# Row scores of both attentions made ten heads ahead, their maxima turned in two parts, and the first stage of the program put in another order

## The chip, the cores and the metric

One core of one Trainium2 chip runs the whole program. The metric is the device time of one execution in microseconds (us), start to end; lower is better. The kernel before was timed in three runs.

## The reference, cut to what matters

Input x is 8 x 100 x 256 (800 rows), the context is 8 x 361 x 256. Four blocks follow each other, each added to x with a gate: an attention, a feed-forward block with fake quantisation, a second attention, and a mixture of eight experts.

```
x = x + tanh(g_xattn[0]) * attention0(layernorm(x), ctx)      # 16 heads of 16, keys: own 100 rows + 361 of the context
x = x + tanh(g_ffn[0])   * quantised_ffn(layernorm(x))        # 256 -> 704 -> 256
x = x + tanh(g_xattn[1]) * attention1(layernorm(x), ctx, ctx) # 16 heads of 16, keys: 361 of the context
x = x + tanh(g_ffn[1])   * experts(layernorm(x))              # 8 experts, best two per row

attention: w = q @ k.T / 4 (with masks); p = softmax(w); a = p @ v; a @ w_proj + b_proj
```

The softmax subtracts each row's maximum. The change is in how and when that maximum is made and used, and in the order of the work that comes before the first attention.

## The kernel before, in words

Every engine has its instruction stream written out by hand, in the order in which it runs; semaphores tie them together. Products that need accuracy are made in three fp16 products of high and low halves (`split3`, L211 to L216). A product lands in PSUM, ScalarE (ACT) copies the high half, VectorE (DVE) makes the low half and thereby frees the bank. PSUM has eight banks: two of them make a "wide" tile (`wide`, used in a cycle of four in the first stage), and in the attention banks 0 and 1 hold row scores, 2 and 3 column scores, 4 (and 5) head values, 5 to 7 are `misc`.

**First stage** (up to the first column scores, L467). The rows x are normalised and turned (L250, L237), the queries, own keys and own values are projected (tiles 2 to 7, `project_T`), weights of the second attention are turned (L936, tiles 8 and 9), then for batch entries 0 and 1 the context is turned (`pe_T`, L393) and projected to the keys of both attentions (`pe_K`, four products each: `share` is where their halves go, L518, L559), then to values (`pe_V`). Queries and keys go out to DRAM scratch and come back as stacks `QS` and `KS`, one slot of 65 rows per head (SyncE's queue, `sp_stack0`). ACT lays head rows (L822): 16 rows behind the stack of `KS` with a constant in head h's row, so that a product with 16 rows of negated maxima in `QS` subtracts the maximum of its own head.

**Rounds.** One round is one batch entry; there are 8 rounds in each attention. For the entry of the round (`o`), step t of 16 (12 in the second attention) makes the scores of four heads by columns (`pe_ST`, L467), ACT takes their exponentials (L530) into PT, and the head values are made from these (`pe_PV`, L495). TensorE (PE) makes in the same steps, for the next entry, the row scores of one head (`pe_SM`, L436 and L439), whose maximum DVE takes (L578, L581) into `mx`. In the first attention a step can also hold a piece for the entry after next (`TVK`: T, K or V). At the end of the round the 16 columns of `mx` are turned (`pe_N`, L448), and ACT lays them in `QS` in two parts, heads 0 to 3 and heads 4 to 15 (`act_max_rows`, L540); `pe_ST` waits for part 0 at step 0 and for part 1 at the group after. The order of each engine is that of the loop bodies `round0` and `round1`; nothing else schedules it.

Bank use sets two more orders: `pe_N` writes to `misc[2]`, where `pe_T` turns the second half of a context tile, so `pe_T` with kc 1 waits for the maxima to be laid (`s_nm`). A row score waits until the maximum of the head two before it is taken (`s_smf`), since there are two banks.

## Time and profile before

| what | us |
|---|---|
| runs of before, median (lowest to highest) | 669.93 (668.5 to 672.32) |
| profiled execution: span, first to last instruction | 664.1 |
| first stage, up to the first column scores (L467) | 80.8 |
| first attention, 8 rounds | 190 |
| out-projection and quantised block | 62 |
| second attention with its projections | 156 |
| experts | 175 |
| PE busy in the span | 515.1 |
| DVE busy | 429.5 |
| ACT busy | 297.8 |

The stages are read off the timeline and rounded. The time of the profiled execution itself is shown only as its span of 664.1 us; the median of the three runs is 5.8 us more than that span, which is what lies around the first and the last instruction together with the difference between executions. A busy PE is not PE at its peak: matmuls overlap, and their ends are modelled.

### The profile page before, as it was taken

To read this page: it belongs to the slowest core of one execution; us is meant where nothing else is said; L and a number is where in the kernel's file an instruction comes from. 1 tells how busy PE (TensorE), PEld (TensorE's weight loads), DVE (VectorE), ACT (ScalarE), POOL (GpSimd) and SP (SyncE) were. 2 spreads that over 40 slices of the span, in tenths; PEclk is the share of its full clock that TensorE was granted. 3 is DMA by queue.
4 is the path that set the end of the run, shared out by engine and by line. 5 is a ranking of instruction groups with operands and counts; after the bars stand their busy time and mean duration, and the time that the engine had idled before them with its cause. 6 is when DMAs were issued, how large, how long until landed. Compare 5 with 4: busy or idle time off the path is not lost. (4 is left out here: it accounts for less than half of the span.)

```text
span 664.1 us, 15475 instructions
## 1 busy us (share of the span) xinstructions
PE 515.1 (78%) x5403; PEld 356.1 (54%) x5403; DVE 429.5 (65%) x921; ACT 297.8 (45%) x482; POOL 162.6 (24%) x191
## 2 busy tenths in 40 slices
PE   2477798998988898737547878998975269999994
PEld 1263365665666667523223545655654258887782
DVE  7365576667686774387754856777569875666662
ACT  6442145556556538203314546676753223333331
POOL 5500022122122211010045410122125044444432
PEclk9989588979999977668659788999976569999997
DMA  9136834444535700000073787789347111222210
GB/s 258 40 120 113 161 82 105 105 115 110 112 99 140 188 5 25 1 1 0 0 154 88 181 155 151 142 165 178 121 158 270 60 40 28 48 40 47 49 19 1
DMA packets 73247, 64.31 MB, mean 97 GB/s; under 512 B 33326, under 2 KB 65750, under 8 KB 73190
## 3 DMA queue, kind: packets, MB, share of 16 engines
q1 hardware_dynamic: 61544, 41.37, 28.3%
q0 software_dynamic: 8224, 21.06, 12.0%
q10 hardware_dynamic: 3424, 1.12, 0.8%
q8 instruction: 37, 0.61, 0.4%
q14 instruction: 18, 0.15, 0.1%
HBM read 48.59 MB, written 15.92 MB: 97 GB/s over the span
## 5 line engine op out<-in xcount | busy, mean ns | idle before, releaser
L467 PEld LDWEIGHTS PS<-QS,KS 112*120 112x120 f16 (+2 forms) x896 | 81.9, 144 | 29.9 <-issue 10.9
L467 PE MATMUL PS<-QS,KS 112*120 112x100 f16 (+2 forms) x896 | 92.8, 229 | 5.1 <-ACT PT L530 3.7
L578 DVE CUSTOM_DVE_ANT_0 PS<-PS,maskv 100x461 f32<-100x461 f32 x128 | 80.5, 647 | 15.2 <-PE PS L436 14.3
L581 DVE TENSOR_REDUCE mx<-PS 100x1 f32<-100x361 f32 x128 | 63.6, 529 | 35.8 <-PE PS L439 34.7
L530 ACT ACTIVATE PT<-PS 120x400 f32<-120x400 f32 (+1 forms) x128 | 63.4, 503 | 45.5 <-PE PS L467 43.1
L530 ACT ACTIVATE PT<-PS,ctxb 120x400 f32<-120x400 f32 (+1 forms) x96 | 57.0, 596 | 52.7 <-PE PS L467 51.9
L436 PE MATMUL PS<-KS,QS 65*100 65x461 f16 x128 | 52.6, 416 | 17.9 <-DVE mx L578 17.3
L795 POOL TENSOR_SCALAR_AFFINE_SELECT PT<-PT 100x400 f32<-100x400 f32 x32 | 17.7, 553 | 187.6 <-ACT PT L530 187.6
L2025 PE MATMUL PS<-aT,WE 128*128 128x128 f16 x960 | 59.4, 224 | 0.0
L2025 PEld LDWEIGHTS PS<-aT,WE 128*128 x960 | 57.0, 101 | 0.0
L2038 PE MATMUL PS<-WE,hidden_high 128*128 x160 | 53.0, 379 | 0.0
L439 PE MATMUL PS<-KS,QS 65*100 65x361 f16 x128 | 43.0, 366 | 11.7 <-DMA QS<-q_scratch 8.2
L1940 ACT ACTIVATE hidden_high<-aall 128x512 f16<-128x512 f32 x40 | 25.1, 630 | 52.8 <-DVE aall L2204 52.8
L1897 POOL DMA_INDIRECT out_dram<-aT,slot_tokens x20 | 31.7, 1584 | 66.5 <-DVE aT L2225 58.6
L1675 PE MATMUL PS<-xn 128*128 128x512 f16 x120 | 44.2, 400 | 2.1 <-DVE xn L277 2.1
L2040 PE MATMUL PS<-WE,hidden_low 128*128 x160 | 43.6, 272 | 0.0
L2204 DVE TENSOR_TENSOR aall<-PS,b1c 128x512 f32<-128x512 f32 x40 | 27.5, 691 | 23.6 <-PE PS L2025 23.5
L540 ACT ACTIVATE QS<-PS 16x400 f16<-16x400 f32 (+1 forms) x32 | 25.4, 821 | 35.3 <-PE PS L448 35.1
L250 PE MATMUL PS<-ident,xn 128*128 128x128 f32 (+1 forms) x56 | 15.5, 425 | 28.4 <-DVE xn L237 25.6
L1512 DVE SCALAR_TENSOR_TENSOR WE<-share,WE 128x2048 f16<-128x2048 f32 (+1 forms) x13 | 31.9, 2451 | 6.4 <-ACT WE L1502 3.5
L559 DVE SCALAR_TENSOR_TENSOR share<-PS,bcol,share 128x361 f16<-128x361 f32 x32 | 19.0, 593 | 24.2 <-ACT share L518 23.2
L439 PEld LDWEIGHTS PS<-KS,QS 65*100 65x100 f16 x128 | 16.6, 132 | 32.9 <-DVE mx L581 19.1
(307 smaller groups left out, 1069.7 us busy)
## 6 DMA issues: line engine op xcount, KB each, us to landing
share<-in_L_ffn_w_dram POOLq DMA_DIRECT2D x13, 1024.0 KB, 9.3
k_scratch<-share SPq DMA_DIRECT2D x32, 180.5 KB, 2.5
KS<-k_scratch SPq DMA_DIRECT2D x32, 180.5 KB, 3.6
KS<-k_scratch SPq DMA_DIRECT2D x64, 90.2 KB, 6.3
QS<-q_scratch SPq DMA_DIRECT2D x64, 50.0 KB, 2.7
v_scratch<-xn SPq DMA_DIRECT2D x8, 385.7 KB
values_staged<-v_scratch SPq DMA_DIRECT2D x8, 385.7 KB
WE<-in_L_ffn_w_dram POOLq DMA_DIRECT2D x2, 1024.0 KB, 8.6
```

Of the source, the lines that this page charges most:

```text
L436: nc.tensor.matmul(bank[0:T, 0:S0], QS[p][0:KROWS + 1, h, :], KS[p][0:KROWS + 1, h, :], start=True, stop=True).then_inc(s_smd, 1)
L439: nc.tensor.matmul(bank[0:T, 0:TC], QS[p][0:KROWS + 1, h, :], KS[p][0:KROWS + 1, h, 0:TC], start=True, stop=True).then_inc(s_smd, 1)
L467: last = nc.tensor.matmul(bank[0:kn, i * T:(i + 1) * T], KS[p][:, h, k0:k0 + kn], QS[p][:, h, :], start=True, stop=True)
L530: nc.scalar.activation(PT[0:kn, c, g * HG:(g + 1) * HG, :].rearrange("p h t -> p (h t)"), st_bank[t % 2][0:kn, 0:HG * T], ACT.Exp, scale=S ...
L578: nc.vector.tensor_tensor_reduce(rows, rows, maskv[:, :], 1.0, -BIG, ALU.add, ALU.max, mx[p][:, h:h + 1]).then_inc(s_smf, 1)
L581: nc.vector.tensor_reduce(mx[p][:, h:h + 1], sm_bank[h % 2][0:T, 0:TC], X, ALU.max).then_inc(s_smf, 1)
L1512: nc.vector.scalar_tensor_tensor(out=lo, in0=in_blocks(raw, m), scalar=WS, in1=hi, op0=ALU.mult, op1=ALU.subtract).then_inc(s_wlo, 1)
L1675: nc.tensor.matmul(misc[1], qh1[:, 0, 0:P], qh1[:, 0, 0:512], start=True, stop=True)
L1897: nc.gpsimd.indirect_dma_start(out=of[:, :], out_offset=bass.IndirectOffsetOnAxis(ap=idx[:, a:a + 1], axis=0), in_=ysb[a % 2], in_offset=N ...
L2025: last = nc.tensor.matmul(WB[a % 2][:, f, :], weights(ready, m, o0, o0 + P), xgT[a % 2][:, l, kc, :], start=(f % HF == 0 and kc == 0 and m ...
L2038: nc.tensor.matmul(YB_[a % 2], hh[a % 2][:, f, :], second(ready, f, 2 * D), start=(f == 0), stop=False, skip_group_check=True)
L2040: nc.tensor.matmul(YB_[a % 2][:, 0:D], hl[a % 2][:, f, :], second(ready, f, D), start=False, stop=False, skip_group_check=True)
```

## The change

1. First stage. ACT lays the head rows in quarters (`head_rows`), most of them later. The nine small loads go from ACT's queue to SyncE's. Context turns and key products of entries 0 and 1 are laid between the projections; tiles 2 to 9 cycle through two wide tiles (banks 0 to 3) and not four. The first ten heads' row scores use four banks (`pe_SM0`, `dve_max0`).
2. Rounds of both attentions: a round's first six steps make the row scores of heads 10 to 15 of its own entry, the rest heads 0 to 9 of the next (`HA = 10`).
3. The maxima are turned in two parts, heads 0 to 7 (step 14; step 10 in the second attention) and all 16 (step 6; step 4) of the next round, into a strip of bank 7 of its own (`max_rows`), and ACT lays 8 heads each time, in 8 and in 16 rows. `pe_T` no longer waits for `s_nm`. In the last round of the first attention the weight turns start one step later.

```diff
+        NW = 10
+        def wide_of(n):
+            return wide[n % 2 if n < NW else n % 4]
+        max_rows = PS[0:H, 7, 512 - T:512]
...
-        SM0 = (0, 5, 10, 16)
+        SM0 = (4, 6, 8, 10)
+        HA = 10
+        NT2, NT1 = 6, 14
+        NSB = 4
...
-            if kc == 1 and o >= 2:
-                pe.wait_ge(s_nm, 2 * (2 * j + o - 1))
...
+        def pe_SM0(pe, h):
+            if h % HM == 0:
+                pe.wait_ge(s_ks[0][h // HM], 16 * 6)
+            if h >= NSB:
+                pe.wait_ge(s_smf, h - NSB + 1)
+            nc.tensor.matmul(PS[0:T, h % NSB, 0:S0], QS[0][0:KROWS + 1, h, :], KS[0][0:KROWS + 1, h, :],
+                             start=True, stop=True).then_inc(s_smd, 1)
...
-            pe.wait_ge(s_smf, 2 * H * j + H * (o + 1) + smn)
-            nc.tensor.transpose(misc[NB][0:H, 0:T], mx[p][:, :], ident[0:T, 0:T]).then_inc(s_nd, 1)
+            p, n = o % 2, HM * (part + 1)
+            pe.wait_ge(s_smf, 2 * H * j + H * o + n + smn)
+            nc.tensor.transpose(max_rows[0:n, :], mx[p][:, 0:n], ident[0:T, 0:T]).then_inc(s_nd, 1)
...
-            if t in (0, nch):
-                pe.wait_ge(s_nm, 2 * (2 * j + o) + 1 + t // nch + nmc)
+            if t in (0, 2 * nch):
+                pe.wait_ge(s_nm, 2 * (2 * j + o) + 1 + t // (2 * nch) + nmc)
...
-            act.wait_ge(s_nd, 2 * j + o + 1 + nmc)
-            hs = slice(0, HG) if part == 0 else slice(HG, H)
-            nc.scalar.activation(QS[p][IROW:KX, hs, :], misc[NB][0:H, 0:T].unsqueeze(1).to_broadcast([H, n, T]),
+            n = HM * (part + 1)
+            act.wait_ge(s_nd, 2 * (2 * j + o) + part + 1 + nmc)
+            nc.scalar.activation(QS[p][IROW:IROW + n, part * HM:n, :],
+                                 max_rows[0:n, :].unsqueeze(1).to_broadcast([n, HM, T]),
...
@@ PE, round of the first attention
-                        if nxt:
-                            pe_SM(pe, j, u + 1, t, 0, 0)
+                        if t < H - HA:
+                            pe_SM(pe, j, u, HA + t, 0, 0)
+                        elif nxt:
+                            pe_SM(pe, j, u + 1, t - (H - HA), 0, 0)
+                        if t == NT2:
+                            pe_N(pe, j, u, 1, 0)
+                        if nxt and t == NT1:
+                            pe_N(pe, j, u + 1, 0, 0)
...
-                        pe_N(pe, j, u + 1, 0, None)
@@ second attention
-        SMH1 = [2, 1, 2, 2, 1, 2, 2, 1, 2, 1, 0, 0]
+        SMH1 = [2, 1, 2, 1, 2, 1, 2, 2, 1, 2, 0, 0]
+        NT2_1, NSTEP1 = 4, 10
...
-                for h in range(H):
+                for h in range(HA):
                     pe_SM(pe, 0, 0, h, 1, SMN)
```

SyncE's stream in the first stage, in words: the nine small loads follow the context of entry 1; the keys of entry 0 go out before the own keys; the context of entry 2 is fetched after the stacks of entry 0 and not before.

**ACT, start of the program.** Before (L822 lays head rows into `KS`, L825 makes the high half of w_attn, L267 that of the turned rows, L269 those of queries and own keys):

```order
L822 ACTIVATE KS<-delta 16x7376 x2
L825 ACTIVATE wah<-PT 128x1536
L267 ACTIVATE xT<-PS 128x800 x2
L835 DMA gts<-in_g_xattn_dram 128x2
...
L269 ACTIVATE qh<-PS,bcol 128x800 x2
L269 ACTIVATE aT<-PS,bcol 128x800 x2
L843 ACTIVATE wrh<-PT 128x512
```

And with the change (L853, L859, L274, L526 for a turned context, L866, L276 in their place):

```order
L853 ACTIVATE KS<-delta 16x1844
L859 ACTIVATE wah<-PT 128x1536
L853 ACTIVATE KS<-delta 16x1844
L274 ACTIVATE xT<-PS 128x800 x2
L526 ACTIVATE cTh_70<-PS 128x361 x2
L866 ACTIVATE wrh<-PT 128x512
L867 ACTIVATE wvh<-PT 128x2x256
L868 ACTIVATE wph<-PT 128x512
L276 ACTIVATE qh<-PS,bcol 128x800 x2
L533 ACTIVATE share<-PS,bcol 128x361 x2
```

A quarter of one stack's head rows stands before the weight copy, where both whole stacks stood; six more quarters come later in the stream.

**PE, steps 5 to 7 of a round of the first attention.** Before (L436 row scores, L467 column scores, L495 head values; REGISTER_ALU and ISA rows left out):

```order
L436 MATMUL PS<-KS,QS_52 100x461
...
L467 MATMUL PS<-QS_53,KS 120x100 x4
...
L436 MATMUL PS<-KS,QS_52 100x461
...
L495 MATMUL PS<-PT,VSB_82 32x100 x4
L495 MATMUL PS<-PT,Vc_62 32x100 x12
...
L467 MATMUL PS<-QS_53,KS 120x100 x4
```

With the change (L444, L482, L463, L510 in their place):

```order
L444 MATMUL PS<-KS,QS_53 100x461
...
L482 MATMUL PS<-QS_53,KS 120x100 x4
...
L444 MATMUL PS<-KS,QS_52 100x461
...
L463 MATMUL PS<-ident,mx_55 16x100
...
L510 MATMUL PS<-PT,VSB_82 32x100 x4
L510 MATMUL PS<-PT,Vc_62 32x100 x12
...
L482 MATMUL PS<-QS_53,KS 120x100 x4
```

The row score of step 5 is now that of the round's own entry (QS_53), head 15, and the turn of all 16 maxima, which needs that head's maximum, stands two products behind it and ahead of the head values.

## Rows read from the trace of the kernel before

**Rows 1.** Windows: busy us (x instructions) by PE, PEld, DVE, ACT, POOL; PE clock, DMA, GB/s.
```profile
10.71:24.93 14.22, 3.96 (x14) 2.59 (x15) 7.31 (x11) 11.91 (x5) 12.88 (x8) 1.00 0.64 185
24.93:42.00 17.07, 17.07 (x112) 12.13 (x112) 8.96 (x18) 6.27 (x11) 1.11 (x1) 1.00 0.30 97
42.00:62.74 20.74, 13.80 (x68) 7.34 (x68) 9.62 (x21) 7.55 (x15) 0.43 (x1) 0.84 0.38 76
62.74:80.78 18.04, 12.81 (x31) 4.79 (x29) 12.55 (x38) 0.55 (x2) 0.00 (x0) 0.60 0.90 155
```
**Rows 2.** Timeline of ACT, first stage: start, us, what.
```profile
7.10 12.58 ACT L822 ACTIVATE KS<-delta 16x7376 f16<-16x7376 f16 x2
19.71 1.48 ACT L825 ACTIVATE wah<-PT 128x1536 f16<-128x1536 f32 x1
```
**Rows 3.** Timeline of PE, first stage; in brackets idle before, and releaser.
```profile
10.71 3.96 PE L250 MATMUL PS<-ident,xn 128*128 128x128 f32 x14 [10.71 <-DVE xn L237]
24.93 0.58 PE L214 MATMUL PS<-xT,wah 128*128 128x512 f16 x1 [10.26 <-DVE xT L275]
...
44.88 0.81 PE L393 MATMUL PS<-ident,share 121*128 121x121 f32 x6 [2.87 <-issue]
...
80.78 0.58 PE L467 MATMUL PS<-QS,KS 112*100 112x100 f16 x4 [0.58 <-ACT QS L540]
```
**Rows 4.** Timeline of DVE, first stage.
```profile
22.90 1.88 DVE L275 TENSOR_TENSOR xT<-PS,xT 128x800 f16<-128x800 f32 x2
```
**Rows 5.** Timeline of SyncE's queue, first stage: issues of DMAs.
```profile
35.08 3.08 SPq L615 DMA_DIRECT2D own_key_scratch<-aT  x4
```
**Rows 6.** Windows (columns as rows 1) of rounds 2 and 3, first attention.
```profile
130.00:155.80 25.80, 23.40 (x270) 15.92 (x262) 16.24 (x47) 13.62 (x25) 4.52 (x9) 0.87 0.43 105
155.80:178.80 23.00, 20.44 (x265) 14.34 (x261) 16.20 (x46) 13.40 (x25) 4.52 (x9) 1.00 0.47 115
```
**Rows 7.** Timeline of PE, round 4.
```profile
181.00 0.53 PE L393 MATMUL PS<-ident,share 121*128 121x121 f32 x3 [0.63 <-ACT QS L540]
183.56 0.40 PE L436 MATMUL PS<-KS,QS 65*100 65x461 f16 x1 [0.90 <-DVE mx L578]
187.02 0.40 PE L436 MATMUL PS<-KS,QS 65*100 65x461 f16 x1
```
**Rows 8.** Timeline of DVE and ACT, round 4.
```profile
187.09 0.59 DVE L559 SCALAR_TENSOR_TENSOR share<-PS,bcol,share 128x361 f16<-128x361 f32 x1
187.60 0.64 DVE L578 CUSTOM_DVE_ANT_0 PS<-PS,maskv 100x461 f32<-100x461 f32 x1
179.79 1.16 ACT L540 ACTIVATE QS<-PS 16x1200 f16<-16x1200 f32 x1
```
**Rows 9.** Timeline of PE and DVE, start of the second attention's rounds.
```profile
359.41 0.51 PE L439 MATMUL PS<-KS,QS 65*100 65x361 f16 x2 [0.59 <-DMA QS<-q_scratch]
369.54 0.65 PE L467 MATMUL PS<-QS,KS 112*121 112x100 f16 x4 [0.58 <-ACT QS L540]
368.49 2.48 DVE L1512 SCALAR_TENSOR_TENSOR WE<-share,WE 128x2048 f16<-128x2048 f32 x1
```
**Rows 10.** Timeline of PE, rounds 1 and 2 of the second attention.
```profile
386.56 0.54 PE L439 MATMUL PS<-KS,QS 65*100 65x361 f16 x2 [2.79 <-DMA QS<-q_scratch]
394.48 0.50 PE L439 MATMUL PS<-KS,QS 65*100 65x361 f16 x2 [1.01 <-DMA QS<-q_scratch]
409.37 0.51 PE L439 MATMUL PS<-KS,QS 65*100 65x361 f16 x2 [1.57 <-DMA QS<-q_scratch]
```
**Rows 11.** Windows (columns as rows 1) of rounds 1, 2 and 3, second attention.
```profile
383.70:402.20 18.50, 14.29 (x179) 9.51 (x179) 10.77 (x20) 9.77 (x17) 1.82 (x2) 0.91 0.68 139
402.20:419.30 17.10, 15.29 (x179) 10.12 (x177) 10.88 (x20) 9.77 (x18) 1.61 (x2) 0.80 0.70 140
419.30:432.70 13.40, 13.00 (x178) 8.12 (x177) 10.58 (x20) 9.77 (x18) 2.78 (x2) 1.00 0.94 176
```

**Rows 12.** Page, DMA issues: count, KB each, median us from issue to landing.
```profile
QS<-q_scratch SPq DMA_DIRECT2D x64, 50.0 KB, 2.7
```

More of the change, by code:

```diff
@@ L264, in wide_hi @@
             act.wait_ge(s_wd, n + 1)
-            src = wide[n % 4][:, 0:NT]
+            src = wide_of(n)[:, 0:NT]
             if bias is None:
@@ L912, in _ @@
                     transpose_rows(pe, kc, kc, 0)
+                for kc in range(KC):
+                    pe_T(pe, 0, 0, kc, kc)
                 pe.wait_ge(s_split, 1)
@@ L1058, in _ @@
                         last = nc.vector.scalar_tensor_tensor(
-                            out=lo, in0=wide[n % 4][:, 512 * i:512 * i + 512].rearrange("p (k n) -> p k n", k=KC),
+                            out=lo, in0=wide_of(n)[:, 512 * i:512 * i + 512].rearrange("p (k n) -> p k n", k=KC),
                             scalar=WS, in1=hi, op0=ALU.mult, op1=ALU.subtract)
                     last.then_inc(s_wf, 1)
+                for k in range(2, 4):
+                    dve_lo_K(dve, 0, 0, k, 6 + k, 6 + k)
                 dve.wait_ge(s_zero, 1)
@@ L1650, in _ @@
                     act_step_part(act, E - 1, 0, 1, q)
-                for part in range(2):
-                    act_max_rows(act, 0, 0, part, NBN)
+                act_max_rows(act, 0, 0, 0, 2 * B)
                 def round1(j, o, first, nxt, e, m, full):
@@ L1733, in round1 @@
                 def round1(j, o, first, nxt, e, m):
-                    for h in range(H):
-                        if nxt:
-                            dve_max(dve, j, o + 1, h, 1, SMN)
-                        if h == 7 and not first:
+                    for h in range(HA, HA + H):
+                        if h < H:
+                            dve_max(dve, j, o, h, 1, SMN)
+                        elif nxt:
+                            dve_max(dve, j, o + 1, h - H, 1, SMN)
+                        if h == HA + 7 and not first:
                             dve_norm(dve, j, o - 1, NBN)
```

227 lines of the change are left out of this document (133 added, 94 removed).

## Prediction, made before the change was timed

> **What bounds the kernel now.** I read the page's slices first, then windows by stage, then the timelines of PE, DVE, ACT and SyncE in the stages that the change touches. The kernel is a chain of stages with different limits, so the total says little; three stages matter.
>
> *First stage, 0 to 80.78 us.* PE turns the rows and then stands idle for 10.26 us [rows 3]. It waits for DVE's low halves of these rows, DVE waits for ACT, and ACT is busy with head rows for 12.58 us, so that its copy of the weights starts at 19.71 [rows 2]; the last low half ends at 24.78 [rows 4]. From there PE is nearly full up to 42 and then works 13.80 of 20.74 and 12.81 of 18.04 us [rows 1], the last stretch at a mean granted clock of 0.60, between its levels of 1.2 and 2.4 GHz. That stretch holds the 16 row scores of entry 0, paced by 16 maxima on DVE, beside value products, and only behind the last maximum is anything turned and laid.
>
> *Rounds of the first attention.* In rounds 2 and 3 PE is busy for 23.40 of 25.80 and 20.44 of 23.00 us [rows 6]. PE is the bound, with small gaps. In round 4, as an example, a context turn waits 0.63 us for the maxima to be laid, and the row score of step 3 waits 0.90 us for a maximum [rows 7]; both hang on ACT, which lays 12 heads in 1.16 us just where the round starts [rows 8].
>
> *Second attention.* Ten us pass between the first row score and the first column score, 359.41 to 369.54 [rows 9]. Rounds 1 and 2 take 18.50 and 17.10 us where round 3 takes 13.40 [rows 11]; three waits for queries, 2.79, 1.01 and 1.57 us, stand in them [rows 10], and their clocks are 0.91 and 0.80.
>
> The quantised block and the experts are the same code, so I cost them at nothing: what leads into them is the same data at an earlier time.
>
> **First stage, part by part.** (a) *Head rows.* 12.58 us for eight quarters is 1.57 each [rows 2]. One quarter in front ends at 7.10 + 1.57 = 8.7. The weights' copy (1.48) then waits for its load, at the latest in time for about 11; the second quarter ends at about 12.3. The rows are turned at 10.71 + 3.96 = 14.67 whatever ACT does [rows 3]. Two high copies and low halves (1.88 for the pair, [rows 4]) behind them let the projections start at about 16.6, not 24.93: 8.3 us less.
>
> (b) *The path behind it.* PE's work from there to the first column score is what the windows from 24.93 hold: 17.07 + 13.80 + 12.81 = 43.7 us [rows 1], some of it at the low clock. Six of the 16 row scores leave; the stretch of 18.04 us holds 16 of them and 12 value products, and with 0.6 us for each of these, its low-clock price, a row score with its maximum is (18.04 - 7.2) / 16 = 0.68 us, so 4 us go (they come back in rounds, below). That leaves 39.7. At the high clock throughout I would get about 30. I take 33, as fewer gaps stand between products. To this come waits that I find by laying the new order out with the durations of the old: weight turns of the second attention to the end of their split (2.9 before, [rows 3]; 2.4 now), a wait of about 1.4 for DVE before the first value product, 1.0 before the last, since DVE also takes maxima there, and 1.3 for turning and laying at the end; together 6. So the first column score comes at 16.6 + 33 + 6 = about 56.
>
> (c) *What could be late instead.* The stacks' DMAs: the own keys' DMAs are now issued at about 30 to 32 (35.08 to 38.16 before, [rows 5]), those of entry 0's stacks follow at once and not at 55, so they have landed by about 45; row scores begin at about 43 for heads 0 to 7, and heads 8 and 9 come behind 48. The nine small loads lie on SyncE's queue at 11 to 15 us, ahead of anything but the queries at 22: no cost. The four quarters of entry 1's head rows, 6.3 us, lie on ACT behind the last key copies, and the first turn of maxima waits for them. This ends within a microsecond of DVE's maxima, so it is the next thing to bind: a bound from below for the stage of 52 to 53.
>
> So 80.78 - 56 = **24.8 less**. Bounds: 52 if nothing but that ACT chain binds (28.8 less), and 66 if the low clock of the last window stays for the whole stretch behind 42 (14.8 less).
>
> **Rounds of the first attention.** Removed: the 0.63 wait, and about half of the 0.90 (DVE's first low half still waits for ACT's copies). Added: one more turn of maxima (two for one), which costs some 0.2 on PE. And PE waits in step 6. The turn needs head 15's maximum. In round 4's timeline the low half of step 5 begins at 187.09, the maximum behind it at 187.60 and ends at about 188.2, while PE is ready for the turn at about 187.2 [rows 7, 8]. That is a wait of **1.1 us, with the head values and all later column scores queued behind it**. In step 14 the same costs about 0.3. The sum is -0.63 - 0.45 + 0.2 + 1.1 + 0.3 - 0.2 (the old turn) = +0.3 per round for rounds 1 to 6; ACT's two layings are 8 heads each, near the old total. Round 0 had no waits at its start to lose: +1.5. The last round gets six more row scores and maxima but loses its jam at the start: 0. Together +3.3. Against it, round 2 lasted 2.8 us more than round 3 at a clock of 0.87 against 1.00 [rows 6]; the low stretches began just behind the gaps at the start that now go. Rounds 0 to 2 have 6 us more than three of round 3's length; I take half of it back. Net **+0.3**, between -5 and +8.
>
> **Second attention.** (d) Six row scores at the 0.6 pace of [rows 9] no longer stand before the first column score: 10.14 us become about 6.5. But DVE's low half of an expert, 2.48 us, now stands between head 9's maximum and head 10's [rows 9], and PE, with two banks, waits for it in step 1: about 1.1 back. Net -2.5. (e) The next entry's first row score moves from step 0 to step 4, and head 8 from step 5 to step 9. A step is some 1.1 us, so both get 4.5 us more for their loads; the waits of 2.79, 1.01 and 1.57 are each shorter than that and go: -5.4, of which I take 1.5 off for loads that start earlier against the same traffic. Rounds 1 and 2 together have 8.8 us more than two rounds like round 3 [rows 11]; what isn't wait is low clock, and of these 3.4 I take half: -1.7. (f) The other rounds gain a little at the turn and lose it by the second one: 0. The last round has six row scores more: +1. Sum **-7**, between 0 and -10.
>
> **Sum.** -24.8 + 0.3 - 7 = -31.5. The profiled span of 664.1 becomes 632.6; the median of the runs is 5.8 above that span, so I forecast 638.4, rounded **639**.
>
> **A rule weighed against this.** What the rows show first: in rounds of the first attention the granted clock is 1.00 or less with gaps of less than 1 us each [rows 6, 7], and a stretch of row scores paced by DVE ran at a mean of 0.60 [rows 1]. The Trainium skill, TensorE: Matmul & The Clock Gate, section "A second HAM failure mode: psum-queue depth-cycling", says that an engine which idles for a moment between groups of products, often enough, keeps swinging between the two clock levels. By it the new waits in steps 6 and 14 would bring the low clock into rounds 3 to 5 too, which is the second rival.
>
> **The rivals.**
>
> *1. The second attention is held by its transfers.* For: DMA engines are busy at 0.94 in the round of 13.40 us [rows 11], so there is little left to gain, and a load started earlier lands no earlier. Against: they were at 0.68 and 0.70 in the rounds with the waits. Then (e) gives nothing and the sum is -24.8 + 0.3 - 2.5 + 1 + 1.7 (waits at other heads) = -24.3: 646. The Trainium skill, DMA: Bandwidth & Descriptors, section "Bandwidth", calls transfers under 64 KB bound by their descriptors; a load of queries has 50 KB [rows 12], so by that rule the DMA engines' share falls no further and this rival holds.
>
> *2. The new turn is a new wait, and takes the clock with it.* Every round of the first attention becomes like round 2: 8 x (2.8 + 0.3) = 25 against a sum over the first three rounds of 6 that is already there, so +19; the second attention keeps its gain of 4. Sum -24.8 + 19 - 4 = -10: 660. For: 1.1 us of idle PE in the middle of each round. Against: idle time before and after the change is about equal in a round, and rounds 3 to 5 bore 1.5 us of it.
>
> *3. Slower.* Low clock everywhere that the change touches, one mechanism: PE's work behind 16.6 us at 1.2 GHz is twice the 30, so the first column score comes at 16.6 + 60 + 2 = 79, a gain of 2; the rounds of both attentions lose 19 and 8 x 2 = 16, the second keeps -4. Sum about +29: 699. It decides when the mean clock in the rounds is below about 0.75. Against: the whole span of the rounds 3 to 5 is at 1.00.
>
> *4. The first stage doesn't shorten as laid out,* because two wide tiles make PE wait for ACT and DVE at each of tiles 4 to 9, where four hid it. Each such wait is at most a copy and a low half, some 2 us, and five tiles have it: -24.8 becomes -15 and the forecast 649. For: DVE also has the splits in front. Against: context products now lie between most of these tiles.
>
> **How the numbers follow.** Forecast (between 630 and 645) 0.55; rival 1 0.15; rival 4 0.15; rival 2 0.10; rival 3 0.02; a larger gain than the bounds 0.03. The range for 8 in 10 leaves out rival 3, most of rival 2 and the edges: 627 to 655. No measurement of this kernel tells a change of under about 0.5% (3.3 us) from none. Faster: all cases but rival 3 and the far edge of rival 2, 0.96; same 0.02; slower 0.02.
>
> **What the profile would show.** Right: the first projection product at about 17 us, the first column score at 53 to 60; in rounds of the first attention no wait of a context turn for ACT, but one of the maxima's turn for DVE in each round, of about 1 us; rounds 3 to 5 at 23.0 to 23.6; in the second attention a first column score 6 to 7 us behind the first row score, and rounds 1 and 2 under 15.5 with no wait for queries over 1 us. Wrong: a first column score behind 62; rounds 3 to 5 with clocks under 0.95; or a wait for queries in steps 4 or 9.

## The result, and the profile after

The changed kernel runs in **635.0 us** (median of 4 runs, 633.37 to 636.21) against 669.21 for the kernel before (4 runs, 661.99 to 672.32): ratio 0.9541, 95% interval 0.9492 to 0.9589. The forecast was 639.0, range 627 to 655. The profiled execution took 633.37 us with a span of 631.6, at a mean granted clock of 0.879 (before: 664.1, 0.861). Timed again in the last of the experiments, beside 11 runs of the kernel before, the ratio was 0.9532 [0.9488, 0.9576].

By stages of the two traces, in us:

| stage, from ... to | before | after | change | forecast |
|---|---|---|---|---|
| start, first column score | 80.78 | 56.12 | -24.66 | -24.8 |
| first attention | 190.08 | 194.94 | +4.86 | +0.3 |
| quantised block and projections, first row score of the second attention | 88.55 | 87.29 | -1.26 | 0 |
| first column score of the second attention | 10.13 | 6.18 | -3.95 | -2.5 (with the wait behind it) |
| second attention | 119.25 | 112.29 | -6.96 | -4.5 |
| the rest (experts) | 175.3 | 174.8 | -0.5 | 0 |

*First stage.* Windows of after, with busy time as in [rows 1]:
```profile
16.52:42.00 25.48, 22.66 (x146) 15.81 (x147) 19.12 (x32) 13.53 (x19) 9.79 (x4) 0.99 0.50 123
42.00:56.12 14.12, 11.20 (x50) 6.04 (x48) 9.96 (x31) 9.88 (x11) 0.00 (x0) 0.90 0.83 136
```
The timeline of PE there (start, us, what, in brackets the idle time before it and what ended it):
```profile
16.52 0.59 PE L221 MATMUL PS<-xT,wah 128*128 128x512 f16 x1 [0.65 <-DVE xT L282]
...
41.15 0.33 PE L221 MATMUL PS<-cTh,w1k 128*128 128x361 f16 x1 [2.83 <-DVE wpl L1117]
...
48.91 0.43 PE L221 MATMUL PS<-wvh,cTh 128*121 128x512 f16 x1 [1.43 <-DVE share L574]
...
53.08 0.43 PE L221 MATMUL PS<-wvh,cTh 128*120 128x512 f16 x1 [0.58 <-DVE xn L585]
...
56.12 0.39 PE L482 MATMUL PS<-QS,KS 112*100 112x100 f16 x4 [0.91 <-ACT QS L554]
```
The projections start at 16.52 where they stood at 24.93 [rows 3]. PE is busy for 33.86 of the 39.60 us from there to the first column score; before it was 43.68 of 55.85 [rows 1]. The last stretch before the first column score has a clock of 0.90 for the 0.60 of before.

*First attention.* Two rounds, then the last one and three parts of it:
```profile
103.70:127.00 23.30, 20.43 (x276) 14.46 (x266) 16.19 (x47) 13.29 (x25) 4.51 (x9) 1.00 0.49 116
127.00:152.00 25.00, 22.14 (x274) 15.29 (x266) 16.14 (x47) 13.29 (x25) 4.51 (x9) 0.93 0.44 107
...
223.50:251.00 27.50, 22.38 (x243) 17.58 (x242) 13.46 (x35) 14.86 (x27) 4.30 (x8) 0.69 0.06 16
223.50:230.00 6.50, 3.68 (x34) 2.31 (x33) 6.09 (x21) 5.68 (x12) 2.01 (x4) 0.94 0.23 61
230.00:238.00 8.00, 7.58 (x67) 6.35 (x68) 2.47 (x5) 5.12 (x8) 0.23 (x1) 0.50 0.01 2
```
PE's waits in the round from 103.7, and in the last round:
```profile
107.35 0.40 PE L444 MATMUL PS<-KS,QS 65*100 65x461 f16 x1 [0.70 <-DVE mx L593]
112.14 0.25 PE L463 MATMUL PS<-ident,mx 100*16 100x100 f32 x1 [0.94 <-DVE mx L593]
...
230.42 1.12 PE L1012 MATMUL PS<-ident,share 128*128 128x128 f32 x4 [2.63 <-DVE share L1202]
```
No context turn waits for ACT any more [rows 7]; L463 is the new turn of step 6, which waits 0.94 us for head 15's maximum. Of two rounds with the same work one takes 23.3 us and the other 25.0, at clocks of 1.00 and 0.93. In the last round PE waits 2.63 us for gate weights that DVE rounds between maxima (DVE is busy for 6.09 of 6.50 us), and works at half clock behind that. In the trace of experiment 12, the same kernel again, the wait is the same and the round is over 4 us shorter (PE, then the window of the round):
```profile
229.71 1.12 PE L1012 MATMUL PS<-ident,share 128*128 128x128 f32 x4 [2.63 <-DVE share L1202]
```
```profile
222.60:246.00 23.40, 18.24 (x251) 14.16 (x244) 13.51 (x37) 14.76 (x27) 4.30 (x8) 0.85 0.07 18
```
So these 4 us go with the clock, 0.69 for 0.85, and not with the wait.

*Second attention.* PE, DVE and POOL at its start, and the window of round 0:
```profile
344.53 0.65 PE L482 MATMUL PS<-QS,KS 112*121 112x100 f16 x4 [0.91 <-ACT QS L554]
...
350.38 0.51 PE L447 MATMUL PS<-KS,QS 65*100 65x361 f16 x1 [3.36 <-DVE mx L596]
...
343.94 5.85 DVE L1578 SCALAR_TENSOR_TENSOR WE<-share,WE 128x2048 f16<-128x2048 f32 x1
...
343.58 4.06 POOL L1549 TENSOR_TENSOR w1k<-share,w1k 2x2048 f16<-2x2048 f32 x1
```
```profile
344.50:362.60 18.10, 14.46 (x151) 9.79 (x151) 14.08 (x18) 9.00 (x16) 7.33 (x5) 0.69 0.75 173
```
DVE's low half of an expert takes 5.85 us for the 2.48 of [rows 9], and PE waits 3.36 us in step 1 where I had 1.1. Round 0, at a mean clock of 0.69, is longer than before the change: 18.0 us for 13.6. Rounds 1 to 6 then take 12.9 to 13.8 us (18.5, 17.1 and 13.4 in [rows 11]), and this trace has no wait for queries like those of [rows 10].

### The profile page after: what moved, and what is told of

It reads as the page before. It is cut to its first block and busy times, and to the rows that moved or that the text cites. A ratio compares the mean times of both kernels' runs of the same rounds, so it can differ in the third digit from the quotient of the medians.

```text
span 631.6 us, 15492 instructions
## 1 busy us (share of the span) xinstructions
PE 499.7 (79%) x5419; PEld 352.0 (56%) x5419; DVE 432.2 (68%) x921; ACT 296.7 (47%) x488; POOL 165.1 (26%) x191
## 5 line engine op out<-in xcount | busy, mean ns | idle before, releaser
L482 PEld LDWEIGHTS PS<-QS,KS 112*120 112x120 f16 (+2 forms) x896 | 81.7, 141 | 26.3 <-issue 10.5
L482 PE MATMUL PS<-QS,KS 112*120 112x100 f16 (+2 forms) x896 | 90.4, 226 | 3.8 <-ACT QS L554 1.8
L593 DVE CUSTOM_DVE_ANT_0 PS<-PS,maskv 100x461 f32<-100x461 f32 x118 | 74.4, 647 | 21.9 <-PE PS L444 21.5
L825 POOL TENSOR_SCALAR_AFFINE_SELECT PT<-PT 100x400 f32<-100x400 f32 x32 | 17.3, 542 | 172.7 <-ACT PT L545 172.7
L444 PE MATMUL PS<-KS,QS 65*100 65x461 f16 x118 | 45.0, 382 | 13.4 <-DVE mx L593 12.9
L2012 ACT ACTIVATE hidden_high<-aall 128x512 f16<-128x512 f32 x40 | 25.1, 630 | 47.8 <-DVE aall L2276 47.8
L447 PE MATMUL PS<-KS,QS 65*100 65x361 f16 x128 | 39.5, 347 | 6.3 <-DVE mx L596 4.4
L2276 DVE TENSOR_TENSOR aall<-PS,b1c 128x512 f32<-128x512 f32 x40 | 27.5, 691 | 18.6 <-PE PS L2097 18.4
L1578 DVE SCALAR_TENSOR_TENSOR WE<-share,WE 128x2048 f16<-128x2048 f32 (+1 forms) x13 | 35.2, 2708 | 6.9 <-ACT WE L1568 4.2
L554 ACT ACTIVATE QS<-PS 8x800 f16<-8x800 f32 (+1 forms) x32 | 26.4, 824 | 24.0 <-PE PS L463 23.8
L1950 POOL DMA_INDIRECT gathered<-rows_scratch,slot_tokens x20 | 27.9, 1394 | 25.5 <-DVE slot_tokens L2247 19.7
```

The source lines that it names most:

```text
L444: nc.tensor.matmul(bank[0:T, 0:S0], QS[p][0:KROWS + 1, h, :], KS[p][0:KROWS + 1, h, :], start=True, stop=True).then_inc(s_smd, 1)
L447: nc.tensor.matmul(bank[0:T, 0:TC], QS[p][0:KROWS + 1, h, :], KS[p][0:KROWS + 1, h, 0:TC], start=True, stop=True).then_inc(s_smd, 1)
L482: last = nc.tensor.matmul(bank[0:kn, i * T:(i + 1) * T], KS[p][:, h, k0:k0 + kn], QS[p][:, h, :], start=True, stop=True)
L593: nc.vector.tensor_tensor_reduce(rows, rows, maskv[:, :], 1.0, -BIG, ALU.add, ALU.max, mx[p][:, h:h + 1]).then_inc(s_smf, 1)
L1578: nc.vector.scalar_tensor_tensor(out=lo, in0=in_blocks(raw, m), scalar=WS, in1=hi, op0=ALU.mult, op1=ALU.subtract).then_inc(s_wlo, 1)
```

## Experiments

Kernels are compared by their ratio to the kernel before in runs beside them; its median was 665.86, 662.47 and 667.42 us in the three groups (runs 1 to 4, 5 to 8, 9 to 12). "Second attention" is measured from its first column score, as in the table.

**1. The first stage alone.** All 16 row scores ahead, and one turn a round, in both attentions:
```diff
-        SM0 = (4, 6, 8, 10)
-        HA = 10
+        SM0 = (4, 8, 12, 16)
+        HA = 16
...
-        SMH1 = [2, 1, 2, 1, 2, 1, 2, 2, 1, 2, 0, 0]
+        SMH1 = [2, 1, 2, 2, 1, 2, 2, 1, 2, 1, 0, 0]
```


> The first stage alone: the new first stage (head rows in quarters, new order, two wide tiles), but all 16 row scores of entry 0 are in it, and both attentions have the rounds of before (16 row scores a round ahead, one turn of maxima at the end). Theory (parts add up): the six row scores that come back cost 4 us, so the first column score stands at about 60 and not at 56; the first attention lasts 190 us as before, the second 119. Span about 664 - 20.5 = 643.5, median about 648. The 4.9 us by which the first attention of the changed kernel is longer than before (194.9 for 190.1) then belong to the moved row scores, its last round above all. Rival (an earlier start costs the rounds): the first attention lasts 195 us here too, and the median is about 653.

Measured: 0.9573 [0.9478, 0.9668]. First column score at 60.48 (60 expected), first attention 189.07 (190), second 115.92 (119, with a sum of 7.2 us of waits for queries and the same code as before). The parts add up: the six row scores are worth 4.4 us in the first stage, and the longer first attention goes with the moved row scores and turns, not with the early start.

**2. The second attention as before**, the rest changed: the SMH1 of experiment 1, and
```diff
-                for h in range(HA):
+                for h in range(HA1):
                     pe_SM(pe, 0, 0, h, 1, SMN)
-                pe_N(pe, 0, 0, 0, SMN)
+                pe_N(pe, 0, 0, 1, SMN)
```
with HA1 = 16, and in its rounds one turn, behind step 10, with both layings.

> The changed kernel, its second attention alone as before: 16 row scores a round ahead, one turn, both layings behind step 10. Theory: the waits of step 0 and step 5 for queries (1.0 to 2.8 us) come back, and six row scores stand again before the first column score: the second attention goes from 112.3 us back to about 119, the median from 635 to about 642. Rival (those waits and low clocks of before hung on where the program stood and not on the order): the second attention stays under 115 us and the median under 638.

Measured: 0.9705 [0.963, 0.9779]. 10.47 us from the first row score to the first column score, and 127.13 us in the second attention, with waits for queries of 3.62, 2.81, 1.18, 0.61 and 2.89 us: the theory holds, with a size (8 us more than the 119 expected) that shows how far these waits vary between traces.

**3. The head rows alone**, in the kernel before: one quarter in front, three behind the own keys' copies, four behind the other weights' copies.
```diff
-                for p in range(2):
-                    nc.scalar.activation(KS[p][IROW:KX, :, :], delta[:, :].unsqueeze(2).to_broadcast([H, H, S0]), ACT.Copy
-                                         ).then_inc(s_kr, 1)
+                head_rows(0, 0)
...
                     wide_hi(act, 4 + mb, skh[:, mb, :], bcol[:, 1, mb:mb + 1])
+                for q in range(1, H // HG):
+                    head_rows(0, q)
```


> The kernel before with one part of the change alone: of the eight quarters of head rows one stands in front on ACT, three behind the own keys' copies, four behind the copies of the attention's other weights. Theory: the projections start at 16.6 and not at 24.9; the three quarters (4.7 us) then make the split of the next weights late by 1 to 2 us, and the first column score comes 6 to 8 us earlier than 80.78, the median at 661 to 663. Rival (what is behind is paced by something else, the maxima on DVE or the low clock): less than 3 us are left of it at the first column score, the median is above 666, and the gain of the first stage is in its order and not in the head rows.

Measured: 1.0066 [1.0021, 1.011]; the first column score stands at 81.35. The rival holds. PE, then ACT:
```profile
19.59 0.59 PE L214 MATMUL PS<-xT,wah 128*128 128x512 f16 x1 [5.15 <-DVE xT L275]
...
48.27 1.44 PE L393 MATMUL PS<-ident,share 121*128 121x121 f32 x6 [11.25 <-issue]
...
31.02 4.99 ACT L823 ACTIVATE KS<-delta 16x1844 f16<-16x1844 f16 x3
37.92 6.62 ACT L823 ACTIVATE KS<-delta 16x1844 f16<-16x1844 f16 x4
```
Here 5.3 of the 8.3 us come at the start; the rest needs DVE's scaling of biases out of the way too (it waited 2.08 us for its load ahead of the low halves), which the change also does. Then PE stands 11.25 us, since the same 11.6 us of head rows lie on ACT in front of the copies (from 44.57) that this order needs next. So moving the head rows gains nothing in the order of before; my reading is that the gain lies in having context products for PE and DVE while ACT lays them. Two things stay untested: the new order with the head rows still in front, and the old order with entry 1's four quarters (6.62 us) behind those copies.

**4. POOL waits for DVE.** One line more in the changed kernel:
```diff
             pool.wait_ge(s_cr, 3)
+            pool.wait_ge(s_wlo, 1)
             nc.gpsimd.tensor_tensor(b2p[0:2, :], stg[0][0:2, :], b2p[0:2, :], ALU.subtract).then_inc(s_b2, 1)
```


> The changed kernel with one wait more: before its subtraction of the second biases (2x2048, 4.06 us) POOL waits for the end of DVE's low half of the expert. Theory (DVE and POOL hold each other up): DVE's low half takes 2.3 to 2.5 us at the same place, not 5.85, PE's wait of 3.36 us in step 1 of round 0 becomes 0 to 0.5, and the second attention ends 3 us earlier: 109 us for 112.3, the median about 632. Rival (the low half is slow for another reason, such as its load or its size): it stays at 5.8 and nothing changes but POOL, which is 6 us later. Second rival: it gets short, but the load that POOL issues behind it makes a later step wait, and the second attention stays at 112.

Measured: 0.9623 [0.954, 0.9707], no gain, and 115.80 us in the second attention for 112.29. DVE, POOL, ACT and PE:
```profile
338.04 2.28 DVE L1579 SCALAR_TENSOR_TENSOR WE<-share,WE 128x2048 f16<-128x2048 f32 x1
...
340.48 4.06 POOL L1550 TENSOR_TENSOR w1k<-share,w1k 2x2048 f16<-2x2048 f32 x1 [2.52 <-DVE WE L1579]
...
351.26 1.06 ACT L1569 ACTIVATE WE<-share 128x1024 f16<-128x1024 f32 x1 [4.34 <-DMA share<-in_L_ffn_w_dram]
...
352.76 0.64 PE L482 MATMUL PS<-QS,KS 112*120 112x100 f16 x4 [1.66 <-ACT PT L545]
```
The theory is right on the cause and wrong on the time (115.80 us lie within the 112.3 to 121.2 that the changed kernel's own code took in four traces, below; that nothing is gained is read from the ratio and the waits). DVE's low half takes 2.28 us and PE's 3.36 are gone. But the load of the next expert stands on POOL's queue behind the subtraction, ACT waits 4.34 us for it behind step 5, and the exponentials queue behind that: the second rival. Also, PE without the wait worked at half clock up to about 360 (0.50 from 338.6 to 355), where in after it was back at 1.00 from 356.

**5. The turns behind the head values**, in the first attention:
```diff
-                        if t == NT2:
-                            pe_N(pe, j, u, 1, 0)
-                        if nxt and t == NT1:
-                            pe_N(pe, j, u + 1, 0, 0)
                         if t in PVT0:
                             pe_PV(pe, j, u, PVT0.index(t), 0, 0, 0)
+                        if t == NT2:
+                            pe_N(pe, j, u, 1, 0)
+                        if nxt and t == NT1:
+                            pe_N(pe, j, u + 1, 0, 0)
```


> The changed kernel, in the first attention the turns of maxima stand behind the head values of steps 6 and 14 and no longer ahead of them. Theory (PE's wait for head 15's maximum, 0.67 to 1.49 us in every round, is on the path, and the head values of step 6 can cover it): the wait in step 6 goes to under 0.2 us, nothing else waits longer, and each of 7 rounds is 0.7 us shorter: -5 us in all. Rival (the maxima are then laid later on ACT, and the column score of step 8 waits for that): a new wait of 0.5 us or more in step 8, and 0 to -1 us. Rival for the clock: rounds 3 and 5 of the changed kernel (24.9 us for 23.3) stay or go, so that the sum moves by up to 3 us either way, without any wait to explain it.

Measured: 0.9424 [0.9366, 0.9482]; first attention 183.49 us. PE's turn of step 6 and the column score of step 8, and the windows of two rounds:
```profile
85.07 0.25 PE L463 MATMUL PS<-ident,mx 100*16 100x100 f32 x1
86.31 0.38 PE L482 MATMUL PS<-QS,KS 112*100 112x100 f16 x4 [0.58 <-ACT QS L554]
```
```profile
102.90:125.60 22.70, 20.29 (x263) 14.40 (x263) 16.19 (x47) 13.37 (x26) 4.51 (x9) 1.00 0.57 133
125.60:148.30 22.70, 20.32 (x263) 14.41 (x263) 16.11 (x47) 13.37 (x26) 4.51 (x9) 1.00 0.47 117
```
The wait is gone from rounds 0 to 5 (0.11 us at most are left there; in round 6, 0.66 of the 1.49 in the first trace); 0.58 us of it come back in step 8 in this round, and in the following ones nothing over 0.55 does. The rounds take 22.7 us for 23.3 and 25.0, and up to 194 us, six rounds, every window is at 1.00. This held in all four traces with the edit: 183.49, 184.20, 184.30 and 184.80 us for the first attention, against 190.1 to 194.9 in the six without it. Seven rounds times the 0.6 us of a round at full clock are some 4 us of the mean 8.3; most of the rest is the low stretches that are gone from rounds 0 to 5. Rounds 6 and 7 keep theirs.

**6. The last round, first attempt.** DVE's six maxima first, then the rounding, then the normalisation; weight turning from step 7.
```diff
-                dve_max(dve, B // 2 - 1, 1, HA, 0, 0)
+                for h in range(HA, H):
+                    dve_max(dve, B // 2 - 1, 1, h, 0, 0)
                 for ib in range(NIB):
...
+                dve_norm(dve, B // 2 - 1, 0, 0)
                 for k, (m, kc, ibs) in enumerate(WPIECES):
...
-                        if weights and 5 <= t < 5 + len(WPIECES):
-                            turning(t - 5)
+                        if weights and t >= 7:
+                            turning(t - 7)
```


> The changed kernel, in the last round of the first attention alone: DVE takes its six maxima first and rounds the gate weights behind them, the normalisation last; PE turns the first piece of weights in step 7 and not in step 5. Theory (the last round is 5 us longer than before because PE waits 2.63 us there for DVE and then works at the low clock): the wait of 2.63 us becomes two of at most 0.6 each, and the round goes from 27.5 to 25.5 us; if the low stretch behind it (16 us at a mean of 0.50) goes too, to 22 or 23. Median 2 to 5 us lower than that of the changed kernel. Rival (PE's work of six more row scores is the cost, and the low clock comes anyway): the round stays at 27.

Measured: 0.9605 [0.956, 0.9649], first attention 193.93 us. The wait moved: the head values now wait for the normalisation that I had put last.
```profile
235.11 0.56 PE L511 MATMUL PS<-PT,VSB 100*32 100x100 f32 x8 [2.78 <-DVE aall L614]
```
The last round took 23.7 us, which looks like a success beside the 27.5 of the first trace. But experiment 12 has 23.4 without any edit, and here the round before the last, with its code unchanged, took 26.6 us at a clock of 0.74 (23.1 in the first trace).

**7 and 8. Products that nobody reads**, one behind each of the ten row scores and four behind the turn, without and with the wait of experiment 4:
```diff
                 for h in range(HA):
                     pe_SM(pe, 0, 0, h, 1, SMN)
+                    unread()
                 pe_N(pe, 0, 0, 0, SMN)
+                for _ in range(4):
+                    unread()
```


> The changed kernel with a product that nobody reads behind each of the ten row scores ahead of the second attention, and four behind the turn of maxima. Theory (the first round of the second attention is slow mostly because the granted clock falls to half where DVE's maxima pace PE, not because of the wait of 3.36 us): the clock stays at 1.00 from the row scores to the first column score and in the steps behind it up to the wait; after that wait it may fall again. Round 0 shortens by 1 to 3 us. Rival (the wait itself brings the low clock): 0. Second rival (more work on PE and the low clock all the same): 1 us longer.

> Both: the products that nobody reads, and POOL's subtraction behind DVE's low half (which made that low half 2.28 us for 5.85 and took PE's wait of 3.36 us away, while the clock stayed at half for 7 us longer and ate it). Theory (two costs in one place, and only the removal of both pays): the clock is at 1.00 through round 0, the second attention lasts 104 to 107 us for the 112.3 of the changed kernel. Rival (a full PE at that place is brought down all the same): a low stretch of 8 us or more in round 0 and over 110 us.

Measured: 0.9619 [0.9559, 0.9678] and 0.9597 [0.9549, 0.9645]; second attention 118.06 and 121.77 us. The clock did stay at 1.00 through the row scores and the first steps (the time at half clock in the 38 us from the first row score falls from 13.6 us to 6.8 and 10.2, in windows of 2 us), and nothing came of it: ACT waits 5.74 us for the load in experiment 7, and PE behind it. Round 0 took 19.3 us in experiment 7; in experiments 5 and 6, where DVE's low half was as short and the clock low for 13.6 us, it took 19.1 and 19.3. So the clock alone was not what held round 0. In experiment 7, without the wait of experiment 4, DVE's low half took 2.28 us all the same and POOL's subtraction 6.16: which of them is slow differs between traces.

**9. The high halves later.** Experiment 5, and ACT's two parts of the expert's high half behind steps 8 and 10 of round 0, not 5 and 8:
```diff
-                        if t in HIT1:
-                            act_step_part(act, e, m, full, HIT1.index(t))
+                        hits = (8, 10) if first else HIT1
+                        if t in hits:
+                            act_step_part(act, e, m, full, hits.index(t))
```


> The turns of maxima behind the head values (the first attention then had no low stretch in six rounds: 183.5 us for 194.9), and in round 0 of the second attention ACT makes the two parts of the next expert's high half behind steps 8 and 10 and not 5 and 8. Theory (what was saved at DVE's low half was lost because ACT waited 3.8 to 5.7 us behind step 5 for the weights' load, with the exponentials of step 6 queued behind it): ACT's wait goes to under 1 us, PE's wait of 2.0 to 2.8 us for PT in step 7 goes, and the second attention is 2 to 3 us shorter than in the run without the shift (118.2 us). Median of the ratio about 0.94. Rival (the load comes later still, or DVE's low half is then late and the next round waits for it): the same total, the wait elsewhere.

Measured: **622.61 us, 0.9348 [0.9303, 0.9393]**, the fastest here, and clear of the changed kernel beside it (636.14, 0.9532 [0.9488, 0.9576]). The second attention took 113.63 us. ACT has no wait for the load, and behind round 0 the window shows a full clock:
```profile
345.92 1.05 ACT L1568 ACTIVATE WE<-share 128x1024 f16<-128x1024 f32 x1
...
350.00:443.46 93.46, 86.90 (x1264) 58.43 (x1264) 73.91 (x128) 67.17 (x120) 13.54 (x13) 1.00 0.74 158
```
What the shift itself brings isn't shown. Its ratio overlaps with that of experiment 5 (0.9424 [0.9366, 0.9482], timed in another group and on another chip), so the two aren't told apart. Of the 6.1 us between the spans of their traces, 4.1 stand in the quantised block (83.93 us for 88.05), whose code is the same in both; its clock was 0.736 for 0.692. In the second attention 4.6 us less stand beside 4.4 us of waits for queries that this trace hasn't got. And POOL came first here, as in the changed kernel's first trace, where ACT had no wait for the load either, without the shift:
```profile
328.86 4.05 POOL L1549 TENSOR_TENSOR w1k<-share,w1k 2x2048 f16<-2x2048 f32 x1
...
329.24 5.81 DVE L1578 SCALAR_TENSOR_TENSOR WE<-share,WE 128x2048 f16<-128x2048 f32 x1
```
ACT's wait is a fair test only where DVE came first: 3.8 to 6.2 us without the shift (experiments 4 to 8 and 12), 0.61 and 1.06 with it (10 and 11). Experiment 5, then experiment 10:
```profile
343.75 1.06 ACT L1568 ACTIVATE WE<-share 128x1024 f16<-128x1024 f32 x1 [3.79 <-DMA share<-in_L_ffn_w_dram]
```
```profile
343.79 1.06 ACT L1569 ACTIVATE WE<-share 128x1024 f16<-128x1024 f32 x1 [0.61 <-DMA share<-in_L_ffn_w_dram]
```
So the shift does take ACT's wait away, but rounds 0 and 1 together are no shorter for it: 33.2 us in both 9 and 10, for 32.5 in experiment 5 (in 10 round 0 is 4.0 us shorter than in 5, at 15.1, and round 1 is 4.7 longer).

**10. Eight row scores ahead** in the second attention, on top of 9, with HA1 = 8 for its HA:
```diff
-        SMH1 = [2, 1, 2, 1, 2, 1, 2, 2, 1, 2, 0, 0]
+        SMH1 = [2, 2, 2, 2, 0, 2, 1, 2, 1, 2, 0, 0]
```

> The same, and in the second attention eight row scores instead of ten are made ahead of their round (two in each of steps 0 to 3, the next entry's from step 5). Theory (the waits of 0.7 to 2.3 us for queries that nine of ten traces show in this attention stand at the first row score of the next entry, in step 4, and each step later takes 1.1 us off them): those waits halve, 1 to 3 us in all less than without it, and two row scores fewer stand ahead of the first column score (1 us). Rival (two row scores in each of the first steps run into DVE, 0.53 us for each maximum and the low half of the expert in front): PE's waits for DVE in steps 1 to 3 take it back, 0 or slower by 2 us.

Measured: 0.9449 [0.9396, 0.9503], slower than experiment 9 beside it; second attention 118.40. A miss, and not by the rival: waits for queries, 3.6 us in all, now stand at the row scores of step 5.
```profile
355.91 0.51 PE L447 MATMUL PS<-KS,QS 65*100 65x361 f16 x2 [2.21 <-DMA QS<-q_scratch]
...
427.39 0.51 PE L447 MATMUL PS<-KS,QS 65*100 65x361 f16 x2 [1.36 <-DMA QS<-q_scratch]
```
**11. The last round, second attempt,** on top of 10: experiment 6, with the normalisation between maxima and rounding:
```diff
                 for h in range(HA, H):
                     dve_max(dve, B // 2 - 1, 1, h, 0, 0)
+                dve_norm(dve, B // 2 - 1, 0, 0)
                 for ib in range(NIB):
```

> The same, and the last round of the first attention: DVE's maxima first, then the normalisation, then the rounding of gate weights; PE turns weights from step 7. Theory (the first attempt only moved the wait: 2.78 us of the head values for a normalisation that was put last): no wait above 1.2 us in the last round, 1 to 3 us less than without it. Rival (the low stretches in this round come with the turning of weights whatever is in front of it): under 1 us.

Measured: 0.9437 [0.9386, 0.9487]; first attention 184.80 us for 184.30.
```profile
220.73 0.38 PE L511 MATMUL PS<-PT,VSB 100*32 100x100 f32 x8 [0.93 <-DVE aall L614]
...
223.30 1.12 PE L1013 MATMUL PS<-ident,share 128*128 128x128 f32 x4 [0.76 <-DVE share L1204]
```
The waits are as the theory has them, 0.93 and 0.76 for 2.63, and the round is no shorter (25.7 us for 25.1): the low stretch stood behind them as before. The rival holds.

**12. The changed kernel again.**

> The changed kernel itself, once more and on the same chip as the others. Theory (the trace of the changed kernel was a lucky one in its second attention, 112.3 us, where six variants of it that have the same code there took 115.8 to 121.8, with waits of 0.7 to 2.3 us for queries): 114 to 119 us in the second attention, with one to three waits for queries over 0.7 us, and a ratio to before between 0.950 and 0.962. Rival (those waits came from the edits): 112 to 113 us and no such wait.

Measured: 0.9532 [0.9488, 0.9576]; span of its trace 637.7. DVE, POOL, then ACT and PE:
```profile
339.74 2.28 DVE L1578 SCALAR_TENSOR_TENSOR WE<-share,WE 128x2048 f16<-128x2048 f32 x1
...
339.57 6.37 POOL L1549 TENSOR_TENSOR w1k<-share,w1k 2x2048 f16<-2x2048 f32 x1
...
352.88 1.06 ACT L1568 ACTIVATE WE<-share 128x1024 f16<-128x1024 f32 x1 [4.26 <-DMA share<-in_L_ffn_w_dram]
...
354.38 0.42 PE L482 MATMUL PS<-QS,KS 112*120 112x100 f16 x4 [3.24 <-ACT PT L545]
...
396.38 0.51 PE L447 MATMUL PS<-KS,QS 65*100 65x361 f16 x2 [1.78 <-DMA QS<-q_scratch]
```
The same kernel in another execution: the first attention 190.14 us for 194.94, the second 121.19 for 112.29 (the 114 to 119 that I had is too narrow). The first trace was lucky in the one and unlucky in the other. Sums and differences of a stage are therefore better read over several traces:

| | traces | first attention | waits for queries | second attention |
|---|---|---|---|---|
| order of before | before, 3, 1 | 188.4 to 190.1, mean 189.2 | | |
| new order | after, 12, 2, 4, 7, 8 | 190.1 to 194.9, mean 192.5 | | |
| turns behind head values | 5, 9, 10, 11 | 183.5 to 184.8, mean 184.2 | | |
| order of before | before, 3, 1, 2 | | 7.2 to 11.1 | 115.9 to 127.1, mean 120.8 |
| new order, as it is | after, 12, 5, 6 | | 0 to 4.4 | 112.3 to 121.2, mean 117.2 |

(Waits for queries: the sum of PE's waits over 0.5 us that a load of QS ended, behind the first row score.)

## Why the prediction was right, and where it was not

*First stage: right, in the total and step by step.* Projections at 16.52 (16.6 forecast), PE busy 33.9 us (33), waits of 2.83, 1.43, 0.58 and 0.91 (2.4, 1.4, 1.0, 1.3), first column score at 56.12 (56). Rival 4, two wide tiles, would have shown as waits of about 2 us at tiles 4 to 9; there are none of that kind. One part of the agreement is luck: the 33 us were chosen between 39.7 and "about 30", and the 30 doesn't follow from the rows. The three windows times their clocks are 36.3 us (17.07 + 13.80 x 0.84 + 12.81 x 0.60) before any row score leaves; six of them at 0.40 us [rows 7] make it some 34 at a full clock, and the trace has 33.9 at 0.99 and 0.90. What the forecast did not say is that step (a) is worth nothing by itself (experiment 3).

*First attention: a term mis-sized.* +0.3 forecast, +4.9 in the trace, +3.3 as a mean over traces, inside the bounds. The waits of a round were right: 0.94 in step 6 (1.1), 0.20 in step 14 (0.3), 0.70 in step 3 (0.45). The failed step is "the last round gets six more row scores and maxima but loses its jam at the start: 0". Its six maxima share DVE with the rounding of gate weights, and 2.63 us of wait and a low stretch stand where the jam was: 27.5 us for the 22 of before in that trace, 23.4 in experiment 12. Over the traces of the two orders the last round takes 25.5 us for 21.1, so this term alone, +4.4, is more than the whole +3.3; how much of it is work, wait or clock isn't separated, and experiment 11 shows that taking the wait away doesn't shorten it.

The other rounds were right where the clock was full: 23.26 us for 23.0, +0.26 a round (+0.3). But the 3 us taken back for the clock did not come: low stretches left rounds 1 and 2 and stood in others. Rounds 3 and 5 took 24.9 us each at 0.93, which the prediction had named as a sign of being wrong (rounds 3 to 5 under 0.95). It isn't rival 2 either. Over five rounds at full clock, rounds 1 to 5 have 3.1 to 4.4 us more in the three traces with the order of before, and 1.6 to 3.3 in the six with the new one: the new wait of step 6 did not bring more low stretches, and the old waits' going did not take them away. Experiment 5 takes them away from the first six rounds. I had named that wait as one "with the head values and all later column scores queued behind it" and let it stand, though the head values of that step could cover it.

*Second attention: the sum right, two steps offsetting.* -7 forecast; -10.9 in the first pair of traces, -7.8 as a mean over traces (-4.2 up to the first column score, -3.6 behind it). Step (d) had DVE's low half at 2.48 us, the figure of a place where POOL was in the last 0.32 us of its subtraction [rows 9]:
```profile
364.77 4.05 POOL L1483 TENSOR_TENSOR w1k<-share,w1k 2x2048 f16<-2x2048 f32 x1
```
Ten row scores in front bring it next to the start of that subtraction, and either DVE waits there, or POOL does and with it the load that ACT needs. Where the forecast had 1.1 us, round 0 is 4.5 us longer than before in the first pair, and 5.8 over the traces (19.3 for 13.5). What makes up for it is behind: rounds 1 and 2 are 8.9 us shorter in the first pair (5.6 forecast), and rounds 3 to 6, put at nothing, 3.6. Step (e), that four steps more take the waits for queries away, was right in the first trace (0 us) and for two thirds over all four: 8.4 us on average in the order of before, 2.6 in the new. Waits of this kind stand in step 4 in experiment 12, the prediction's other sign of being wrong. So rival 1 was a part of the truth, but no more: where its loads land no earlier for being started earlier, the waits would not have fallen by two thirds. Experiment 10, a step later still, has 3.6 us of these waits, within the 0 to 4.4 of the others, and shows no gain from it.

*The sum.* -24.7 (one pair of traces) + 3.3 - 7.8 (means) = -29.2, against -31.5. The runs themselves say -34.2 in the first timing (669.2 to 635.0) and -31.3 in experiment 12 (667.4 to 636.1), with ratios of 0.9541 and 0.9532 that agree. That the total came so near is in part luck: a last round and a round 0 that cost some 9 us more than forecast were met by gains in rounds 1 to 6 of the second attention that were put too low.

## What to carry to other kernels

Before a long piece is taken out of the front of a stage, ask what the engines will do while it is done later: in experiment 3, with no new work laid over it, its removal was given back to the last microsecond. Put a turn or a lay-out that waits for the newest result behind the work that doesn't need it; here, when one small wait went from each round, the clock's low stretches went too in the first six, and were worth about as much as the waits. Before a stage is compared between two variants, have a second trace of each: one kernel's stages differed by 5 and 9 us between executions. And where one engine is made to start earlier, look at what the others have there at that time: a duration read from the old place holds only beside the old neighbours.

## What the runs showed of the hardware

*DVE and POOL exclude each other on these two operations.* DVE's low half (two operands in SBUF, 128x2048) takes 2.28 us alone, POOL's subtraction (2x2048) 4.06. In after POOL's begins at 343.58 and DVE's at 343.94, and DVE's ends at 349.79, which is the end of POOL's, 347.64, and 2.15 us. Before the change it is the same: DVE's ends at 370.97, 2.15 us behind the 368.82 of POOL. In experiment 12 DVE's is done in 2.28, at 342.02, and POOL's ends 3.92 us later. The loser waits for the whole of the winner. By the records DVE lost where it began 0.36 and 0.38 us behind POOL (after, experiment 9), and won where it began at most 0.17 us behind, or ahead (experiments 5 to 7 and 10 to 12). The Trainium skill, SBUF — State Buffer, section "SBUF: two separate sides", says this: the pair of ports that the two share is an exclusive lock for the whole instruction, and whichever starts first has it. The traces agree on the lock. On who gets it they don't quite: in experiments 6 and 12 POOL's record begins 0.14 and 0.17 us ahead, and DVE has it all the same (the profiler's times on POOL are rough).

*One order, two outcomes.* The two traces in which POOL won (after, experiment 9) have no wait for queries at all in the second attention, and 112.3 and 113.6 us; those in which DVE had 2.28 us (4 to 8 and 10 to 12) have 0.7 to 5.2 us of such waits, and 115.8 to 121.8. Which came first also decides ACT's wait for the next expert's load, which POOL issues behind its subtraction: none in those two traces, 3.8 to 6.2 us in experiments 4 to 8 and 12. Why the later loads of queries differ I did not find; no run held the winner fixed to POOL, so this stays open.

*The clock does not follow the gaps one by one.* In experiment 4 PE was as good as full from 338.6 to 355 (14.53 of 16.40 us) at a granted clock of 0.50, the lower of its two levels, while after, with a gap of 3.36 us there, was back at 1.00 from 356. In experiment 11 the low stretch of the last round stayed, with two waits of about a third of the old one in front of it. In experiment 12 the last round had a mean clock of 0.85, in the first trace 0.69, both with the same wait of 2.63 us. Only in experiment 5, and in the three that contain it, where the same wait went from each round, are six rounds free of low stretches.
